# Sampling rows interleaved over the partitions, and the column weights finished on another engine

## The reference

```python
off = conv(x, offset_w, stride=16) + offset_b        # for each of 256 kernel points a shift dy, dx
py = base_y + dy;  px = base_x + dx                   # where point k of output (ho, wo) samples
y0 = floor(py);  x0 = floor(px);  wy1 = py - y0;  wx1 = px - x0
sampled = (gather(y0, x0)   * (1 - wy1) * (1 - wx1) + gather(y0, x0+1)   * (1 - wy1) * wx1
         + gather(y0+1, x0) * wy1 * (1 - wx1)       + gather(y0+1, x0+1) * wy1 * wx1)
out = einsum('bhwkc,ock->bohw', sampled, dconv_w)     # 192 channels, 5 x 5 tokens, 32 images
```

## Time and profile before

| | us |
|---|---|
| median of three timed runs | 1320.39 (1316.8 to 1324.31) |
| the profiled execution, by its own time | 1309.12 |
| its span, from first to last instruction | 1307.5 |
| sampling loop, first transfer to the barrier behind it | 72.14 to 257.37 |
| busy over the span: PE / DVE / ACT / POOL | 903.5 / 636.0 / 427.5 / 215.1 |

### The profile page before, as it was taken

How to read it: one execution, slowest core, us unless ns; L and a number is a source line. 1 busy time by engine, 2 the same in 40 slices (tenths; PEclk the granted TensorE clock), 3 DMA queues, 4 the chain that set the end, 5 groups by cost and what they waited for, 6 DMA issues and landing times. The chain is left out here.

```text
span 1307.5 us, 25828 instructions
## 1 busy us (share of the span) xinstructions
PE 903.5 (69%) x9931; PEld 739.1 (57%) x9931; DVE 636.0 (49%) x1464; ACT 427.5 (33%) x728; POOL 215.1 (16%) x240
## 2 busy tenths in 40 slices
PE   4936666654656469828988557857677999476684
PEld 1335555522333359726878556646447999464573
DVE  1637777636776343166444233645463111256354
ACT  0148888512333112123334322334220111133132
POOL 2122222110000134213112001010012332100100
PEclk9969999976665579968888758968586999879598
DMA  4323333276000358010000060000052996100000
GB/s 120 83 87 113 115 114 114 79 191 145 1 0 1 98 174 204 19 49 2 2 2 2 1 156 9 4 1 3 1 133 68 225 256 144 32 2 3 1 4 20
DMA packets 63923, 90.67 MB, mean 69 GB/s; under 512 B 16532, under 2 KB 51016, under 8 KB 63824
## 3 DMA queue, kind: packets, MB, share of 16 engines
q1 hardware_dynamic: 58320, 83.57, 23.4%
q0 software_dynamic: 5504, 5.70, 2.2%
HBM read 81.66 MB, written 8.12 MB: 69 GB/s over the span
## 5 line engine op out<-in xcount | busy, mean ns | idle before, releaser
L1752 PE MATMUL ps_rows<-stage_strip,stage_hat_y 128*128 128x144 f32 x800 | 110.4, 294 | 73.1 <-ACT stage_hat_y L1719 73.1
L1752 PEld LDWEIGHTS ps_rows<-stage_strip,stage_hat_y 128*128 128x128 f32 x800 | 102.1, 193 | 81.4 <-ACT stage_hat_y L1719 50.1
L1783 DVE TENSOR_TENSOR stage_product<-ps_rows,stage_hat_x 128x1296 f32<-128x1296 f32 x80 | 68.9, 902 | 42.8 <-PE ps_rows L1752 42.8
L2559 DVE TENSOR_TENSOR L_ffnhid<-L_ffnact_gate,L_ffnbank_u 128x300 f32<-128x300 f32 x32 | 15.0, 467 | 117.6 <-ACT L_ffnact_gate L2577 117.6
L1791 DVE TENSOR_REDUCE stage_samples<-stage_product 128x1440 f32 x40 | 66.2, 1655 | 9.3 <-DVE stage_product L1783 9.3
L1714 ACT ACTIVATE stage_hat_y<-stage_hat_y,stage_w_minus_row 80x1280 f32<-80x1280 f32 x40 | 54.5, 1362 | 45.8 <-DMA stage_hat_y<-places_y 45.8
L1734 POOL TENSOR_TENSOR stage_hat_x<-stage_pos_xT,stage_w_window_x 128x240 f32<-128x240 f32 x80 | 48.4, 627 | 125.0 <-DVE stage_product L1783 118.9
L1556 PE MATMUL ps_conv<-stage_w_offset_w,stage_patches 128*100 128x512 f32 x96 | 44.8, 620 | 17.6 <-DMA stage_patches<-in_patchesT 17.6
L1719 ACT ACTIVATE stage_hat_y<-stage_hat_y 80x1280 f32<-80x1280 f32 x40 | 50.1, 1253 | 0.0
L1135 PE MATMUL L_attnbank_q<-L_attnhT,L_attnwq 97*128 97x200 f32 x192 | 43.6, 374 | 6.9 <-DVE L_attnqT L1298 6.7
L1135 PEld LDWEIGHTS L_attnbank_q<-L_attnhT,L_attnwq 97*128 97x128 f32 x192 | 36.8, 213 | 9.4 <-issue 8.7
(11 more groups left out here) (430 smaller groups left out, 2176.3 us busy)
## 6 DMA issues: line engine op xcount, KB each, us to landing
stage_hat_y<-places_y SPq DMA_DIRECT2D x40, 400.0 KB
L_ffn_win<-in_L_ffn_Win SPq DMA_DIRECT2D x10, 1152.0 KB, 8.9
stage_L_ffn_win<-in_L_ffn_Win SPq DMA_DIRECT2D x6, 1152.0 KB, 9.2
L_ffnranks<-stage_ranks SPq DMA_DIRECT2D x16, 400.0 KB
L_ffn_win<-in_L_ffn_Win SPq DMA_DIRECT2D x8, 768.0 KB, 14.0
L_ffn_wout<-in_L_ffn_Wout SPq DMA_DIRECT2D x10, 576.0 KB, 6.3
stage_L_ffn_wout<-in_L_ffn_Wout SPq DMA_DIRECT2D x6, 576.0 KB, 6.5
stage_strip<-in_strips SPq DMA_DIRECT2D x160, 19.7 KB
```

Of the source, the lines that this page charges most:

```text
L1752: mm = nc.tensor.matmul(ps[:, p % 2, bank, at * cols:(at + 1) * cols], hat_y[:, p, g, h * P:(h + 1) * P], rhs.rearrange("q j c x -> q (j c ...
L1783: last = nc.vector.tensor_tensor(split(product[:, p % 2, slots.start * cols:slots.stop * cols]), ps[:, p % 2, banks, 0:used * cols].rearra ...
```

## The change

Three things change in `sample`. The 80 pixel rows of the four images are interleaved: row r of image j now lies on partition 4 r + j in place of 20 j + r. For that the source of `places` repeats each set of four images 20 times (the repeat is now the outer dimension, the images the inner one), a strip goes to every fourth partition, and `minus_row` is laid out to fit. Second, ScalarE's Relu of `hat_x` is gone, and GpSimd makes min(x, 1) - 1 instead, which is the same weight with its sign turned; it waits for ScalarE's Abs first. `hat_x_taken` is a count that nobody waits for. Third, VectorE's sum over the columns negates its result.

```diff
                     sp.dma_start(hat_y[0:ROWS_Y, p].rearrange("q w c -> q (w c)"),
-                                 places.unsqueeze(1).to_broadcast([IMG_PER_TILE, WINDOW, GRID * KPOINTS])).then_inc(loads[kind]["places"][p], 16)
+                                 places.unsqueeze(0).to_broadcast([WINDOW, IMG_PER_TILE, GRID * KPOINTS])).then_inc(loads[kind]["places"][p], 16)
                     for j in range(IMG_PER_TILE):
-                        q = slice(WINDOW * j, WINDOW * (j + 1))
+                        q = slice(j, ROWS_Y, IMG_PER_TILE)
...
-                    act.wait_ge(s["hat_x_abs"], n)
-                    nc.scalar.activation(x, x, ACT.Relu, scale=-1.0, bias=1.0).then_inc(s["hat_x"], 1)
...
                     x.then_inc(s["hat_x_sub"], 1)
+                    pool.wait_ge(s["hat_x_abs"], n)
+                    pool.sem_inc(s["hat_x_taken"], 1)
+                    x = hat_x[:, p].rearrange("q w x -> q (w x)")
+                    nc.gpsimd.tensor_scalar(x, x, 1.0, 1.0, ALU.min, ALU.subtract).then_inc(s["hat_x"], 1)
...
-                        nc.vector.tensor_reduce(into.rearrange("q h c w -> q h w c"), by_window, AX_X, ALU.add).then_inc(s["summed"], 1)
+                        nc.vector.tensor_reduce(into.rearrange("q h c w -> q h w c"), by_window, AX_X, ALU.add, negate=True).then_inc(s["summed"], 1)
...
-    o["minus_row"] = -np.resize(np.arange(WINDOW, dtype=np.float32), P)[:, None]
+    o["minus_row"] = -np.repeat(np.arange(QUAD, dtype=np.float32), IMG_PER_TILE)[:, None]
```

More of the change, by code:

```diff
@@ L1635, in sample @@
     nc, ins = tw.nc, tw.ins
-    names = "hat_y_abs hat_y hat_x_sub hat_x_abs hat_x rows_in_psum multiplied summed added".split()
+    names = "hat_y_abs hat_y hat_x_sub hat_x_abs hat_x_taken hat_x rows_in_psum multiplied summed added".split()
     NEAR, FAR = "near", "far"
@@ L1790, in step @@
                     if kind == NEAR:
-                        nc.vector.tensor_reduce(into.rearrange("q h c w -> q h w c"), by_window, AX_X, ALU.add).then_inc(s["summed"], 1)
+                        nc.vector.tensor_reduce(into.rearrange("q h c w -> q h w c"), by_window, AX_X, ALU.add, negate=True).then_inc(s["summed"], 1)
                     else:
-                        nc.vector.tensor_reduce(part[:].rearrange("q h c w -> q h w c"), by_window, AX_X, ALU.add).then_inc(s["summed"], 1)
+                        nc.vector.tensor_reduce(part[:].rearrange("q h c w -> q h w c"), by_window, AX_X, ALU.add, negate=True).then_inc(s["summed"], 1)
                         dve.wait_ge(s["summed"], n)
```

## The result

| | before | after |
|---|---|---|
| median of the runs, us | 1322.35 (4 runs, 1316.8 to 1333.33) | 1350.85 (4 runs, 1345.15 to 1351.89) |
| ratio, with its 95% interval | | 1.0257 (1.021 to 1.0304) |
| profiled execution, us (its span) | 1309.12 (1307.5) | 1351.89 (1350.2) |
| sampling loop in it, us | 185.23 | 216.80 |
| from the loop's end to the end, us | 1050.1 | 1062.1 |

A forecast was written before the change was run, and what follows sets the result against it. The prediction took the DMA of `places`, 4.3 us a step, as the bound, with VectorE's 3.54 next. Saved 27.3 (pace) + 2.1 (first landing) - 1.0 (loop ends) = 28.4 us, from 1320.39 to 1292.0; range 1284 to 1310.

The forecast's parts named there:

- the part on the order of rows: Loop's DMA transfers: interleaved `places` falls to 2.2 us a step on ten engines; strips' issues unchanged, cost nothing.
- SP's free running step: First loop steps: SP issues `places` 3.3 us apart, waiting for nobody, while deliveries come every 4.3 us.
- all three rivals: Loop: `places` transfer no faster (0.10, 1320 us); GpSimd stretching the product (mild 0.12, hard 0.05); dear GpSimd finish (0.03).
- the DMA's 4.3 us: Loop before: transfers of `places`, on four always busy DMA engines, set the pace at 4.3 us a step.
- VectorE is next: Loop after: once `places` is faster, VectorE's product and reduction set the pace, 3.54 us a step.
- The first landing: Loop start: first `places` transfer lands 5.7 us after issue instead of 7.77, 2.1 us earlier (bounds 0 and 3).
- Removing the Relu: ScalarE in the loop: its second Relu, 40 x 0.59 us, hid in the DMA wait; removal alone worth nothing.
- GpSimd's finish: GpSimd's added min and subtract, 128x480, after ScalarE's Abs: 0.6 us (0.43 to 1.25), hidden.
- the ring: ScalarE and GpSimd in the loop: Abs 0.59, finish 0.6, subtractions 1.21, three hops: 2.7 us, covered by VectorE's 3.54.
- Rival 3: GpSimd's min and subtract dear: at 2.3 us the kernel takes 1328 us; decides from 2.1 us on; chance 0.03.
- negate: VectorE's reduction in the loop: negating its result takes the same elements and pass, so 0 us.
- Rival 2: GpSimd's work beside VectorE's product stretches the product: mild to 1312 us, chance 0.12; hard, at most 1339 us, 0.05.

The follow-up runs named there:

- experiment 4: Kernel before with only the order of `places` and `minus_row` interleaved, strips on consecutive partitions (samples wrong): 1290.12 us against 1315.96, ratio 0.9817, loop 154.10 us.
- experiment 1: Kernel before with only the interleaved rows (`places`, strips, `minus_row`), ScalarE's Relu kept: 1352.89 us against 1315.96, ratio 1.0295, loop 216.75 us.
- experiment 5: Kernel before with only the strips sent to every fourth partition, `places` as before (samples wrong): 1343.99 us in one run, loop 215.20 us.
- experiment 6: Kernel before with its four strip transfers in four forms of rows, partition steps and source gaps (samples wrong): 1306.81 us in one run.
- experiment 9: Kernel before, old row order, `places` in four transfers, two of four strips issued by GpSimd: 1281.83 us against 1314.03, ratio 0.9784, loop 153.70 us.
- experiment 10: Kernel before with interleaved rows, Relu kept, two of four strips issued by GpSimd: 1285.28 us against 1314.03, ratio 0.98, loop 155.60 us.
- experiment 2: Changed kernel with the old order of rows, so only GpSimd's finish and the negated sum: 1315.71 us against 1315.96, ratio 1.0008, loop 185.50 us.
- experiment 3: Changed kernel with strips on consecutive partitions, `places` still interleaved (samples wrong): 1296.06 us against 1315.96 before, ratio 0.9852, loop 164.97 us.
- experiment 8: Kernel before in old row order, `places` sent as four transfers, one for each image: 1308.37 us against 1318.84, ratio 0.9934, loop 175.70 us.

## Why the prediction was wrong

**The step that failed** is in the part on the order of rows: "The four strips keep 20 rows each, on every fourth partition: same issues, cost taken as nothing; SP's five issues take 2.7 us of a step, covered up to there." The issues were not the same: 741 ns for 286, 804 for 677, 1.95 us more a step, so that SP was not covered but last, at a measured 5.14 instead of 3.54 us a step. The loop was forecast at 157 us and took 216.8; 39 x (5.14 - 3.54) = 62.4 us accounts for the 59.8 us between them (the 2.6 over are near the 3 us by which the forecast of the loop was long in experiment 4 too).

Two things in the trace of before spoke against it. First, 2.7 us is the stretch from the start of the issue of `places` to the end of the fourth strip's (163.20 to 165.84 in the earlier trace rows); what SP does between that and its next issue is not in it. SP's free running step is 3.3 us, which the prediction worked out itself from the earlier trace rows and then didn't use. With `places` at its new 0.80 that leaves 3.54 - 3.43 = 0.11 us, 0.03 a strip, before SP is the bound, and (4.30 - 3.43) / 4 = 0.22 us a strip before the kernel is slower than it was. A cost taken as nothing needs its break-even beside it, and this one was tiny.

The runs put the margin a little wider. In the four kernels with five issues a step in which SP hardly waits (after, experiments 1, 5 and 6) its step, 5.14, 5.14, 5.07 and 4.20 us, is the sum of the five median prices, 3.77, 3.77, 3.68 and 2.83, and another 1.37 to 1.39. By that experiment 4 should have 0.81 + 4 x 0.286 + 1.37 = 3.33 us, and it has: (133.9 us from first to last issue of `places` - 4.0 of waits) / 39 = 3.33. So the margin measured is 3.54 - 3.33 = 0.21 us, 0.05 a strip.

Second, the trace of before showed that an issue has no fixed price: 0.67 us for `places`, 0.29 for a strip (its line's instructions, above); of what in the two transfers makes that difference, nothing there tells. The nearest row above for a strip of changed form was 0.68. With it the bound is 3.3 + 4 x 0.39 = 4.86 us a step, 39 x 0.56 = 22 us over the old pace, 1342: slower than before, and most of what came. That case stood neither in the range nor among the rivals; all three rivals asked what moves data or computes, none what asks for it.

**What held.** The reading of before: the DMA's 4.3 us were four busy engines, and spreading `places` ends that (experiment 4). That it was four is an inference from the mean share and the count of small packets (below); the traces don't show single DMA engines. VectorE is next, at 3.54 us (experiments 4, 9 and 10). The loop of experiment 4 took 154.1 us, 3 under the 157 forecast. The first landing came 5.33 us after its issue, against a forecast of 5.7 and 7.77 before:

```profile
71.32 1.02 SPq L1691 DMA_DIRECT2D stage_hat_y<-places_y  x1
...
76.65 1.36 ACT L1714 ACTIVATE stage_hat_y<-stage_hat_y,stage_w_minus_row 80x1280 f32<-80x1280 f32 x1 [12.52 <-DMA stage_hat_y<-places_y]
```

**Removing the Relu was worth nothing**, as said (experiments 2 and 4).

**GpSimd's finish was mis-sized.** Forecast 0.6 us, bounds 0.43 to 1.25; measured, with the reduction and the product of after below it:

```profile
L1738 POOL TENSOR_SCALAR stage_hat_x<-stage_hat_x x40: 1811/1812/1852, 78.7 to 278.7; 128x480 f32<-128x480 f32 x40
```

```profile
L1793 DVE TENSOR_REDUCE stage_samples<-stage_product x40: 1654/1655/1656, 87.2 to 286.2; 128x1440 f32 x40
```

```profile
L1785 DVE TENSOR_TENSOR stage_product<-ps_rows,stage_hat_x x80: 296/898/1509, 85.3 to 285.6; 128x1296 f32<-128x1296 f32 x40, 128x144 f32<-128x144 f32 x40
```

1.81 us is 3.8 ns an element, against 0.9 of the copy and 2.6 of the two-input form, both in the earlier trace rows (only this one size was run, so how much of it is a fixed cost is open). The copy was taken because it too reads one input, but two operations with constants are no copy. The upper bound was no bound either: it priced one operation on two inputs, not two operations. It hid behind SP here; without SP's cost it makes the ring 3.81 us (experiment 3), which is the ring the prediction wrote down, at 2.7, with this term wrong. Rival 3's point of decision, 2.1 us, was not reached.

**negate costs nothing**: 1655 ns against 1654 without. **Rival 2 did not happen**: in the timeline of after the finish runs from 150.65 to 152.46 beside a product that starts at 151.54 and takes its usual 1.72 us; all 80 have the durations of before (295/897/1509). By the rule of the Trainium skill, GPSIMD Engine Reference, "Key points", named in the prediction, a product with one input in PSUM doesn't contend with GpSimd; the trace agrees.

**The number of engines.** By the rule of the Trainium skill's DMA: Bandwidth & Descriptors, small packets should go from 44 to 50 a step. The program has 64164 packets after and 63923 before: 240 more on SP's queue, 6 in each of 40 steps, and one elsewhere; the trace agrees. But the share of the DMA engines did not follow the sum. The prediction's 0.38 was 21.8 engine-us of work a step (0.317 x 16 x 4.3) in 3.54 us. Experiment 4 has 0.59 x 16 x 3.54 = 33.4, and after, at 42.3% of 16 engines in 150 to 200 us, 0.423 x 16 x 5.14 = 34.8. If all of the surplus is in the 80 rows of `places`, a row takes about 0.32 us on ten engines where 0.176 was taken from four. I had put 2.2 us a step for ten; by this it is nearer 3.3. The first landing doesn't fit that row price, though: 7.77 - 20 x 0.176 + 8 x 0.32 would be 6.8 us, and it took 5.33. So where the surplus lies is open. Since nothing waited for it, this error cost nothing here, but it was as large as the others.

**The granted clock** in the loop fell to 0.85 (before 0.96), so that TensorE ran a part of the loop at 1.2 instead of 2.4 GHz, and a step there took 4.39 us in the place of 2.72 (granted 0.61 in that stretch; the prediction had put such a step at 5.4). Its waits between steps had grown, from 1.57 us in the earlier trace rows to 2.74 ahead of that step. I take the clock for a consequence. That it is no cause is shown: SP, the bound, never waited for TensorE, and experiment 1's loop is as long, 216.75 us, at a granted clock of 0.81.

## What to carry to other kernels

An engine that only issues DMAs has a pace of its own, which no table of busy time shows: take its free running step from the first steps of a loop, gaps included, and whenever an access pattern changes, on either side and for whatever reason, ask how far each issue may grow before that engine is last. Here the margin was 0.03 us a strip by the rows of before (0.05 measured), and the growth 0.46. And where a layout is changed to spread one transfer, look at what the same layout does to its neighbours: four plain transfers of 20 copies gave the same spread with no interleaving, and half of the strips' issues given to an engine with time to spare gave the gain that was looked for (0.9784 of before).

## What the runs showed of the hardware that was not expected

- SP's issue of a transfer to neighbouring partitions took 286 ns, to every second or fourth partition 741 to 751, for 10 rows as for 20; a source with gaps added 40 ns. GpSimd's issue took 505 to 507 ns in either form. Why SP pays for a skipping destination is open; the runs only give the price.
- The issue of `places` took 674 to 717 ns with the images outermost (the kernels differ in their strips), 803 to 814 with the copies outermost, and 286 for one image's 20 copies. The number of DMA engines doesn't explain it, since by the number of small packets the last uses ten as well; the count of dimensions may, which was not tried alone.
- The DMA engines' busy time for the same bytes a step was 21.8 engine-us with `places` on four engines, 28.7 in four transfers (experiment 8, 43.7% of 16 at 4.1 us) and 33.4 in one interleaved one. That rows of one source read by more engines at once get slower would fit, but strips to every fourth partition with `places` as before also gave more, 28.3 (experiment 5, 35.4% at 5.0 us). So part of it may lie in the strips; this stays open.
- A min and a subtract with constants in one instruction on GpSimd cost 1812 ns for 480 elements a partition, 3.8 ns each, four times the 0.89 of the copy of 3264.
